# A two-layer gated cross-attention and expert kernel: context loaded first, sums cleared elsewhere, the last product split

## What is computed

```python
# layer 0 attention: 16 heads of 16; the last 16 context rows have weights and a softmax of their own
q = _ln((x @ Wq + bq).reshape(b, s1, H, HD), qn_w, qn_b)
kv = concat([y_main @ Wk + bk, y_main @ Wv + bv])      # keys normalized per head
ctx = _attn(q, k, v) + _attn(q, k_dca, v_dca)
x = x + tanh(g_xattn[0]) * (ctx @ Wo + bo)
# layer 0 experts: 32, top 8, a capacity of 512 rows each
probs = softmax(_layernorm(x) @ gate_w); w, sel = top_k(probs, 8); w = w / sum(w)
y[t] += w * (silu(x @ w_gate[e]) * (x @ w_up[e])) @ w_down[e]
# layer 1: attention with 16 heads of 128, then 64 experts (top 4) and 2 shared ones
```

## Time and profile before

| what | us |
|---|---|
| median of 3 runs | 1856.32 (1855.57 to 1856.35) |
| the profiled execution | 1856.43 |
| its span | 1854.7 |

### The profile page before, as it was taken

One profiled execution on the slowest core, in us unless ns is written; L12 is line 12 of the kernel. 1 busy time (PEld: TensorE's weight loads), 2 busy tenths in 40 slices (PEclk: granted clock), 3 DMA queues, 4 the chain that ended last, 5 costly groups with the idle time before them and its releaser, 6 DMA issues. The chain is left out here.

```text
span 1854.7 us, 31886 instructions
## 1 busy us (share of the span) xinstructions
PE 1780.7 (96%) x9204; PEld 1303.2 (70%) x9204; DVE 1401.1 (76%) x2298; ACT 1232.0 (66%) x2094; POOL 485.1 (26%) x425
## 2 busy tenths in 40 slices
PE   5899999999999999999999999999999999999998
PEld 3444444468888667786777767777677777888887
DVE  6576666466666889897989989899799996566665
ACT  4576868842332798888988879888898884222232
POOL 4010101215444640005300063000630002544442
PEclk9899999989999999999999999999999999999999
DMA  3523222345433100000000000000000000554452
GB/s 100 112 50 80 66 64 57 73 173 131 112 106 90 54 18 1 0 0 19 18 1 0 0 19 19 0 0 0 1 23 1 8 9 21 116 116 112 106 119 74
DMA packets 109737, 95.90 MB, mean 52 GB/s; under 512 B 72821, under 2 KB 94201, under 8 KB 109017
## 3 DMA queue, kind: packets, MB, share of 16 engines
q1 hardware_dynamic: 109656, 94.88, 20.3%
HBM read 72.94 MB, written 1.44 MB: 40 GB/s over the span
## 5 line engine op out<-in xcount | busy, mean ns | idle before, releaser
L1111 ACT ACTIVATE s_p<-ps,s_g,s_rk 128x256 f32<-128x256 f32 (+1 forms) x832 | 412.6, 560 | 8.8 <-DVE s_dsum L2220 7.8
L1405 PE MATMUL ps<-s_qq,s_ctxT 128*128 (+3 forms) x1248 | 357.3, 399 | 5.9 <-ACT s_p L1111 3.6
L495 PE MATMUL ps<-s_xT,s_wgus 128*128 128x512 f32 x1440 | 348.5, 390 | 0.0
L1405 PE MATMUL ps<-s_ps,s_ctx 128*128 128x512 f32 x1152 | 324.8, 395 | 1.0 <-DVE s_ps L2211 1.0
L495 PEld LDWEIGHTS ps<-s_xT,s_wgus 128*128 128x128 f32 x1440 | 269.9, 188 | 59.4 <-issue 1.5
L972 ACT ACTIVATE s_p<-ps,s_bsm 128x1024 f32<-128x1024 f32 x208 | 222.6, 1114 | 89.9 <-PE ps L1249 57.2
L2211 DVE TENSOR_TENSOR s_ps<-s_p,s_ps 128x512 fp32r<-128x512 f32 x384 | 268.8, 700 | 17.7 <-ACT s_ps L1121 14.2
L1405 PEld LDWEIGHTS ps<-s_qq,s_ctxT 128*128 128x128 f32 (+1 forms) x1248 | 222.8, 184 | 68.4 <-ACT s_p L1111 12.0
L1405 PEld LDWEIGHTS ps<-s_ps,s_ctx 128*128 128x128 f32 x1152 | 215.7, 188 | 56.5 <-DVE s_ps L2211 4.2
L2220 DVE TENSOR_TENSOR s_dsum<-s_dsum,s_p 128x512 f32<-128x512 f32 (+1 forms) x352 | 241.9, 687 | 16.2 <-ACT s_p L1111 12.7
L393 ACT CAST s_hs<-s_hw 128x512 fp32r<-128x512 f32 x120 | 74.5, 621 | 197.9 <-DVE s_hw L1996 197.9
(11 more groups left out here) (282 smaller groups left out, 2358.5 us busy)
## 6 DMA issues: line engine op xcount, KB each, us to landing
s_wB<-w1s SPq DMA_DIRECT2D x64, 256.0 KB, 3.9
s_kT<-s_kst SPq DMA_DIRECT2D x96, 128.0 KB, 2.4
s_kT<-s_kst SPq DMA_DIRECT2D x96, 80.0 KB, 2.1
s_wB<-w0s SPq DMA_DIRECT2D x15, 384.0 KB, 3.5
s_wB<-w0s SPq DMA_DIRECT2D x16, 256.0 KB, 3.7
s_wgu<-in_L_ffn_Wg_dram SPq DMA_DIRECT2D x64, 64.0 KB, 2.8
s_wgu<-in_L_ffn_Wu_dram SPq DMA_DIRECT2D x64, 64.0 KB, 2.6
s_wd<-in_L_ffn_Wd_dram SPq DMA_DIRECT2D x64, 64.0 KB, 2.4
```

The source lines that it names most:

```text
L495: ins = nc.tensor.matmul(ps[:, 4 + g, :], WGUS[f][:, slot, w, g, k, :], XT[f][:, x_, k, n], start=c == 0, stop=c == len(ops) - 1)
L1111: ins = nc.scalar.activation(p1[0:r, SLOT1[t], j, :], ps[0:r, BANK1[t], j * SQ:(j + 1) * SQ], ACT.Exp, bias=g1[0:r, 3:4], scale=rk_col(t, ...
L1405: ins = nc.tensor.matmul(out, lhs(x_), rhs(y_), start=first and n == 0, stop=last and n == 2)
```

## The change

- Loads: the first four context tiles (FIRST0) come right behind wkv, then bkv and wdca, then x, then bkv's other rows, the rest of the context, wq and bq. The new semaphores ctx_first and bkv_loaded are waited for by TensorE's tile 0 and VectorE's second centering.
- First stage: TensorE projects ten tiles before it transposes x. VectorE's statistics, variance, normalization and third centering are spread between its reads of the tiles; two query reads move behind the scaling of the keys. ScalarE's order follows. GpSimd fills vg batch by batch, and waits for one query read instead of four.
- Entry to experts 0: banks 0 and 1 are cleared before the first half of x is transposed, banks 2 and 3 before the second half's logits; the transposes use banks 4 and 5. gates reads the logits in PSUM without a copy.
- Ends of the expert stages: the last pe_down does its four products with the high part first and waits for the low part only before the last two. Both halves of the sums are kept by ScalarE; in experts 0 this comes before its copy of wk1.

```diff
--- before.py
+++ after.py
@@ -79,6 +79,7 @@
...
 QBANK = (4, 7, 5, 6)
+FIRST0 = 4
...
@@ -322,7 +323,7 @@
...
         S = {n: sem(n) for n in (
-            "vb_loaded v0_read x_loaded gates_loaded w0_loaded small0_loaded ctxT0_loaded "
+            "vb_loaded v0_read ctx_first bkv_loaded x_loaded gates_loaded w0_loaded small0_loaded ctxT0_loaded "
             "router_loaded w1_loaded ctx1_loaded0 ctx1_loaded1 stored "
...
@@ -344,7 +345,8 @@
...
-            return 4 + c if (k, half) == (3, 0) else (4 if k == 2 else 0) + 2 * half + c
+            return 4 + c if k == 1 or (k, half) == (3, 0) else (4 if k == 2 else 0) + 2 * half + c
...
@@ -400,7 +402,10 @@
...
-            act.wait_ge(s.down_done, primed(2 * U0 + 1 if f == 0 else 2 + 2 * U0 + 8 + E1))
+            done = 2 * U0 + 1 if f == 0 else 2 + 2 * U0 + 8 + E1
+            act.wait_ge(s.down_done, primed(done - 1))
+            nc.scalar.copy(yT[:, 0:2, :], ps[:, 0:2, :]).then_inc(s.yT_kept, 1)
+            act.wait_ge(s.down_done, primed(done))
             nc.scalar.copy(yT[:, 2:4, :], ps[:, 2:4, :]).then_inc(s.yT_act, 1)
...
@@ -496,14 +501,21 @@
...
-        def pe_down(pe, u0, i, j, loaded):
+        def pe_down(pe, u0, i, j, loaded, last=False):
             slot, half = unit_half(u0, i, j)
...
                 pe.wait_ge(s.wd_split, loaded)
+            if last:
+                pe.wait_ge(s.hs_hi, primed(at(u0, i, 4, j + 1)))
+                for k in range(KD):
+                    for w in range(2):
+                        nc.tensor.matmul(ps[:, 2 * half + k, :], WDS[f][:, slot, w, k * P:(k + 1) * P], hs[:, j % 2, 0, :],
+                                         start=False, stop=False, skip_group_check=True)
             pe.wait_ge(s.hs_lo, primed(at(u0, i, 4, j + 1)))
             for k in range(KD):
-                for h, w in PRODUCT:
+                for h, w in ((1, 0),) if last else PRODUCT:
                     ins = nc.tensor.matmul(ps[:, 2 * half + k, :], WDS[f][:, slot, w, k * P:(k + 1) * P], hs[:, j % 2, h, :],
...
@@ -565,19 +577,22 @@
...
                 sp.sem_inc(S[name], PRIME)
-            def load_ctx0(b):
-                sp.dma_start(ctxT0[:, 0:KC], a["ctxT"][b][:, 0:KC]).then_inc(s.ctxT0_loaded, 16)
+            def load_ctx0(b, first=0):
+                sp.dma_start(ctxT0[:, first:KC], a["ctxT"][b][:, first:KC]).then_inc(s.ctxT0_loaded, 16)
                 sp.dma_start(ctxT0[:, KC:KC + KREST], a["ctxT"][b][:, KC:KMAIN]).then_inc(s.ctxT0_loaded, 16)
...
             sp.dma_start(wkv0[:], a["Wkv0"]).then_inc(s.wkv_loaded, 16)
+            sp.dma_start(ctxT0[:, 0:FIRST0 * P], a["ctxT"][0][:, 0:FIRST0 * P]).then_inc(s.ctx_first, 16)
+            sp.dma_start(bkv0[:, 0, :], a["bkv0"][:, 0, :]).then_inc(s.bkv_loaded, 16)
+            sp.dma_start(wdca0[:], a["Wdca0"]).then_inc(s.bkv_loaded, 16)
             sp.dma_start(x[:], xf).then_inc(s.x_loaded, 16)
+            sp.dma_start(bkv0[0:DROW, 1, :], a["bkv0"][0:DROW, 0, :]).then_inc(s.bkv_loaded, 16)
+            sp.dma_start(bkv0[DROW:P, 1, :], a["bkv0"][DROW:P, 1, :]).then_inc(s.bkv_loaded, 16)
             sp.wait_ge(s.pad_zeroed, 1)
-            load_ctx0(0)
-            for dst, src in ((bkv0[:, 0, :], a["bkv0"][:, 0, :]), (wdca0[:], a["Wdca0"]),
-                             (bkv0[0:DROW, 1, :], a["bkv0"][0:DROW, 0, :]), (bkv0[DROW:P, 1, :], a["bkv0"][DROW:P, 1, :]),
-                             (wq0[:], a["L0_xattn_Wq"].rearrange("(k p) n -> p k n", p=P)), (bq0[:], a["bq0"])):
+            load_ctx0(0, FIRST0 * P)
+            for dst, src in ((wq0[:], a["L0_xattn_Wq"].rearrange("(k p) n -> p k n", p=P)), (bq0[:], a["bq0"])):
                 sp.dma_start(dst, src).then_inc(s.w0_loaded, 16)
...
@@ -751,19 +766,19 @@
...
             me.did(g_.memset(ones[:], 1.0))
-            me.did(g_.memset(vg[:, :, 0:KT - 1, :], 1.0))
-            me.do(g_.memset(vg[:, :, KT - 1:KT + 1, :], 0.0))
-            me.did(g_.memset(vg[0:32, :, KT - 1, :], 1.0))
             for j in range(2):
+                me.did(g_.memset(vg[:, j, 0:KT - 1, :], 1.0))
+                me.do(g_.memset(vg[:, j, KT - 1:KT + 1, :], 0.0))
+                me.did(g_.memset(vg[0:32, j, KT - 1, :], 1.0))
                 me.do(g_.memset(vg[32:64, j, KT - 1, :], 1.0))
...
                                        base=DCA, pattern=[[0, H0 * (D0 + 1) + D0 - 1]], channel_multiplier=-1))
-            pool.sem_inc(s.vg_ones, 1)
-            pool.wait_ge(s.q0_read, 4)
+                pool.sem_inc(s.vg_ones, 1)
+            pool.wait_ge(s.q0_read, 1)
             for b in range(B):
...
@@ -911,11 +926,6 @@
...
-            act_std(act, 0)
-            act.wait_ge(s.vg_ones, 1)
-            first_values(range(0, 4))
-            for half in range(2):
-                act_take(act, 0, half, (0, 1))
...
@@ -937,10 +947,18 @@
...
-            for c in range(4):
-                if c < 3:
-                    first_values(range(4 * c + 4, min(4 * c + 8, KT)))
-                square(0, c)
+            act.wait_ge(s.vg_ones, 1)
+            first_values(range(0, 7))
+            act_std(act, 0)
+            first_values(range(7, 9))
+            square(0, 0)
+            first_values(range(9, 10))
+            square(0, 1)
+            for half in range(2):
+                act_take(act, 0, half, (0, 1))
+            first_values(range(10, KT))
+            square(0, 2)
+            square(0, 3)
             key_std(0)
...
@@ -1011,10 +1029,10 @@
...
                 return
+            act_keep(act, 0)
             act.wait_ge(s.w1_loaded, 16 * 7)
...
                              for w in (wk1[:, 0, :], stage[:, 0:H1 * D1]))).then_inc(s.wk_hi, 1)
-            act_keep(act, 0)
             nc.scalar.activation(rq1[0:1, 1, 0:1], ones[0:1, 0:1], ACT.Sqrt).then_inc(s.act_steps, 1)
...
@@ -1165,7 +1183,9 @@
...
                 m = MISC["proj", b, t]
-                if t == 0:
+                if (b, t) == (0, 0):
+                    pe.wait_ge(s.ctx_first, 16)
+                if t == (0 if b else FIRST0):
                     pe.wait_ge(s.ctxT0_loaded, 48 * (b + 1))
...
@@ -1252,10 +1272,10 @@
...
             pe.wait_ge(s.w0_centered, 1)
-            for t in range(4):
+            for t in range(10):
                 project(0, t)
             pe_turn_start(pe, 0)
-            for t in range(4, KT):
+            for t in range(10, KT):
                 project(0, t)
...
@@ -1331,9 +1351,13 @@
...
             pe.wait_ge(s.gate_loaded, 16)
+            pe.wait_ge(s.consts_made, 3)
+            pe.wait_ge(s.ln_var, TURN_LN[1] + 1)
+            pe_zero((0, 1))
             pe_turn_half(pe, 1, 0)
...
             pe_turn_half(pe, 1, 1)
+            pe_zero((2, 3)).then_inc(s.down_done, 1)
             gate_logits(1)
...
@@ -1348,9 +1372,7 @@
...
-            pe.wait_ge(s.consts_made, 3)
             positions(0)
-            pe_zero(range(4)).then_inc(s.down_done, 1)
             turn_gates(0)
...
@@ -1382,7 +1404,7 @@
...
                     pe_up(pe, 4 * last, None, j + 1, 2 * last + (j + 1) // 2 + 1)
-                pe_down(pe, 4 * last, None, j, 2 * last + j // 2 + 1)
+                pe_down(pe, 4 * last, None, j, 2 * last + j // 2 + 1, j == 3)
             pe_turn_back(pe, 0)
...
@@ -1623,7 +1645,7 @@
...
                     pe_up(pe, u0 + 8 + 4 * last, None, j + 1, 2 * last + (first + (j + 1) // 2 + 1))
-                pe_down(pe, u0 + 8 + 4 * last, None, j, 2 * last + (first + j // 2 + 1))
+                pe_down(pe, u0 + 8 + 4 * last, None, j, 2 * last + (first + j // 2 + 1), j == 3)
             pe_turn_back(pe, 1)
...
@@ -1721,10 +1743,7 @@
...
             center((0,), s.w0_centered)
-            dve.wait_ge(s.x_loaded, 16)
-            statistics(range(NT))
-            normalize(0)
-            dve.wait_ge(s.w0_loaded, 16 * 6)
+            dve.wait_ge(s.bkv_loaded, 16 * 4)
             center((1, 2), s.w1_centered)
...
@@ -1878,23 +1897,35 @@
...
                 read_projected(0, t)
+                if t == 3:
+                    dve.wait_ge(s.x_loaded, 16)
+                    statistics(range(0, 4))
+                if t == 5:
+                    statistics(range(4, 8))
+                if t == 6:
+                    variance(range(NT))
                 if t == 7:
+                    apply_std(0, range(NT), 0)
+                if t == 8:
+                    dve.wait_ge(s.w0_loaded, 16 * 2)
                     center((3, 4), s.wq_centered)
+                if t == 9:
                     sum_squares(0, 0)
-                if t == 9:
                     columns()
+                if t == 10:
                     bound_squares()
...
                     sum_squares(0, 1)
+            sum_squares(0, 2)
             take_queries(0)
-            sum_squares(0, 2)
             sum_squares(0, 3)
             key_variance(0)
-            for j in range(1, 4):
-                take_queries(j)
+            take_queries(1)
             inverse_std(0)
...
             scale_keys(0, 1)
+            take_queries(2)
```

(10 more changed lines are left out.)

## The result

| kernel | median us | runs |
|---|---|---|
| before | 1857.24 | 12, 1854.94 to 1860.57 |
| changed | 1861.95 | 12, 1859.39 to 1865.70 |

The ratio is 1.0025, 95% interval 1.0017 to 1.0033: slower, by 4.6 us. The forecast was 1855.3 with a range up to 1858.4. The profiled execution of the changed kernel took 1859.84 (span 1858.0), one of its shortest, so its trace shows 3.3 us of the loss.

The account below looks back on a forecast made before the run. TensorE, busy 96% of the span, was taken as the bound, so only its standing still could be won. First stage +0.2, entry +0.1, ends −0.7 each made −1.1: 1856.4 to 1855.3 us, range 1852.2 to 1858.4.

Parts of the forecast that it names:

- The loads: First stage: bkv's last part, needed by VectorE's centering, lands at 11.1 us, with 10.4 and 12.0 as ends.
- my own sign of being wrong: First stage: the forecast is wrong if VectorE's second centering starts before 10 or after 12.5 us.
- The early start is worth nothing: First stage: TensorE starts 4.8 us sooner, but its fifth tile waits for VectorE's first read, so nothing is gained.
- Order of VectorE's work: First stage: read 12 ends 1.0 us later, moved query reads gain a net 0.8, together +0.2 us.
- read 7 behind the root: First stage: VectorE's read 7 waits for ScalarE's tile copy behind its root, a new wait of 0.7 us.
- The clock at the entry: Entry to experts: with the clears moved, the clock rises some 2 us later, costing 0 to 1.1 us, taken as 0.5.
- rival (b): First stage and entry: bkv lands near 10.4 and early clears keep the clock up, giving 1852.0 us; chance 0.10.
- Rival (a): First stage and entry: the clock falls in TensorE's holes and rises late, giving 1857.9 us; chance 0.20.
- The clears "cost 0": Entry to experts: the 1.87 us of clears fit into TensorE's existing waits and so cost 0.
- The ends: Ends of both expert stages: high-part matmuls cover the wait for the low part, −0.7 us each, bounds −0.4 and −0.9.
- Rival (c): Ends of the expert stages: they do not get shorter, giving 1856.6 us, no change; chance 0.10.
- The loops between are untouched: Between the changed places: a gain or loss at a place shifts all that follows one for one.

Follow-up runs that it names:

- e8: The changed kernel with bkv's two halves loaded ahead of x, against the kernel before: 1861.36 us, ratio 1.0028.
- e9: The changed kernel with x loaded behind the rest of the context, against the kernel before: 1858.41 us, ratio 0.9992.
- e1: The kernel before with only the changes at the ends of the two expert stages: 1855.85 us, ratio 0.9994.
- e7: The changed kernel with twelve fp32 matmuls in TensorE's first-stage holes, against the kernel before: 1860.35 us, ratio 1.0013.
- e10: The kernel before with the changes at ends and entry plus eight zero matmuls before the gates' transposes, old first stage: 1856.96 us, ratio 0.9991.
- e4: The changed kernel with eight zero matmuls before the gates' transposes, against the kernel before: 1857.68 us, ratio 1.0002.
- e6: The changed kernel with the four clears put back before the gates' transposes, against the kernel before: 1860.05 us, ratio 1.0016.
- e13: The changed kernel as it is, run again against the kernel before: 1861.90 us, ratio 1.0026.
- e5: The changed kernel as it is, run again against the kernel before: 1862.25 us, ratio 1.0025.
- e2: The kernel before with only the changes at the entry to the experts: 1858.24 us, ratio 1.0011.
- e14: The changed kernel with x loaded behind the context and eight zero matmuls before the gates' transposes, against the kernel before: 1854.52 us, ratio 0.9988.

## Why the prediction was wrong, point by point

- **The loads** ("By bytes it lands at 10.9", taken as 11.1, ends 10.4 and 12.0). bkv's last part landed at about 12.9, outside my ends and beyond my own sign of being wrong (12.5): 1.8 us of the first stage's 3.3. Counting kilobytes up to its end assumed the rate of before and that nothing issued later comes in between. From 2.0 to 10.9 us 264 GB/s were moved, against 304 in the kernel before, and by 12.9 it was 2.8 MB, more than the 2304 KB counted; each half took 7.4 us from issue to landing, against 6.6 in the earlier trace rows. And the step asked only for what VectorE waits for. TensorE's fifth tile also needs the context's last piece, which went from the front of the queue to behind x; e8 showed that it was as late (15.46), e9 what both cost.
- **"The early start is worth nothing"** held: fifth tile at 15.61, TensorE idle 4.50. In this trace it was worse than nothing: right behind the idle time the clock was at 0.50 (16 to 19 us), where e9, with 1.24 us idle, had 1.00.
- **Order of VectorE's work** (+1.0 − 0.8). From the centering to the end of read 12 it took 20.7 us where I had 19.9. The wait that I forecast, read 7 behind the root, was 0.60 (0.7 forecast). The 1.18 at 19.67, read 5, was not forecast, and it is the clock's: TensorE's fifth and sixth tiles ran at half, so ScalarE's copies of them started 1.71 us apart (17.49 and 19.20), in e9 0.86 (13.27 and 14.13). The wait for the last squares was 1.06 (1.2 forecast), and one of 0.52 came that I had not. The reciprocal came at 38.85 against 35.8, 3.1 late: 1.8 for the loads and 1.2 for the rest, and e9 shows that the order as such is no loss.
- **The clock at the entry** (step: "those 2 us at half speed cost 0 to 1.1 us", taken as 0.5). This term failed by the most. I priced a rise that comes 2 us later. What happened is that the clock had risen already at 402, as rival (b) had it, and fell again at 405, for ten microseconds, in the hole that the removed clears left; there it lies on dense products of the chain. 3.2 us in this trace, and about 2 against e1, whose entry is the old one with the clock at half up to 410. In this trace rival (b)'s condition was met and its gain was real (logits 2.13 for 3.62 us, gates 0.8 nearer to the end of the first context stage) but it was given back fourfold. In e7, e8, e9 and e10, with the same early clears, the second logits took 3.59 us.
- **Rival (a)** named both places, with 0.20 and 1857.9. In the first stage the falls came, at 16 and 26 us, the second lasting past 29, which is what this rival needed; my reason against them, that each hole is shorter than the one of 5.2 us, did not hold (4.50 and 2.12 us). At the entry it had my late rise, not a fall, and the price was three times its 1.1. It was the nearest of my cases, and still 4 us short of the median. The Trainium skill has the rule that activity releases the throttle (TensorE: Matmul & The Clock Gate, Part 1), and e4, which added nothing but activity, agrees: PEclk 1.00 for 0.50 at 405 to 415 us.
- **The clears "cost 0"** as time of TensorE, right; as cover of a hole they were worth some 2 us (e6, with intervals that overlap), and a full cover more (e4).
- **The ends**, −0.7 each: measured 0.73 and 0.71, and e1 alone 0.8 us in the median, with an interval that takes in both 1.4 and 0. Rival (c) fell.
- **The second context stage.** "The loops between are untouched, so a gain or loss at a place is taken to shift all that follows one for one" did not hold either: of the 3.3 us at the first scores 2.1 went away, and 1.2 came in between 848 and 1073 us, where nothing was changed. No run was made on this. Of two more executions of the changed kernel e13 has the fall at 852 us and e5 has it not.
- **The sum of parts.** Ends 0.9994, entry 1.0011, first stage 1.0013 make 1.0018 where the whole has 1.0025 and 1.0026. Each has 0.0009 either way, so whether the parts add to each other stays open. So does why the clock falls at 50 us in one execution and at 66 in another. The spread of the runs goes with it: over the 33 executions of the changed kernel on record the time and the mean granted clock have a correlation of −0.80, and the three with a trace took 1859.84, 1860.82 and 1864.18 us with 17.0, 20.4 and 25.5 by the sum above.

## What to carry to other kernels

A hole on TensorE can have two prices: the time itself and half speed for the dense work behind it; so a cheap instruction moved out of the front of a critical wait may have been what closed the hole. When a load is reordered, list for every consumer all loads that it waits for and where each stands now, since a wait for two shows only the later; the large load whose consumer comes last goes last. Where holes can't be closed, matmuls whose sums nobody reads fill them (here about 3 us for eight). And one trace of each kernel is too little to price a place where the clock changes: the same instructions took 9.8 or 10.9, and 10.4 to 14.4 us.

## What was not expected of the hardware

At about the same total of half clock (18.7 and 17.0 us by the sum above) the time went up by more than 3 us in the profiled executions. So between two kernels the total doesn't tell the time; where the half clock lies does, besides the late loads. Being busy didn't bring the clock back at once: in the kernel before it stayed at 0.50 through the whole of the logits at 400.52, 3.62 us of 128x32 products without a gap. In the changed kernel, with two 128x512 clears just ahead of the same logits, it was up within 2 us of the clears' start, and so it was in e2, e4, e5, e13 and e14; but in e7, e8, e9 and e10 the same two clears and logits ran at half throughout. What decides this the runs don't show. Nor did it take a long hole for a fall: at 405 us TensorE had stood for 1.5 us. Loads issued close together landed close together: with x among them, the 24.5 KB and 8 KB pieces of the context took 7.4 us from issue to landing and the 512 KB one 7.6; with x behind, 4.5, 4.8 and 4.7.
